# Second routing re-ordered: late tiles normalised ahead of the first half's choice, halves in turns, ScalarE's functions grouped by table

## The chip, the cores and the metric

The kernel runs on one core of a Trainium2 chip. The metric is device microseconds (us) from start to end, the median of several runs. In the text PE is TensorE, ACT is ScalarE, DVE is VectorE, POOL is GpSimd and SP the engine that issues the DMAs.

## The reference, cut to what matters

Two decoder layers over 4 x 256 = 1024 tokens of 256 features. The second layer is attention, an mLSTM, and a mixture of experts; each is added to its input and layer-normalised. The change lies in what leads from the mLSTM to the second layer's experts, 55 us of the run, and in the last heads of the mLSTM.

```python
x = _layernorm(x + mlstm(x, ctx))                         # head norm of every head, then the layer's norm
scores = softmax(x @ gate_weight.T)                       # 64 scores a token
topk_w, topk_idx = top_k(scores, 6)
w_dense = zeros((T, 64)).at[rows, topk_idx].add(topk_w)
flat = w_dense[:, inv_mapping]                            # [T, 8 experts, 8]
scalar = flat.sum(-1)
soft = softmax(where(flat == 0, -1e9, flat), axis=-1)
...
sh = silu(x @ sh_gate_W.T) * (x @ sh_up_W.T) @ sh_down_W.T   # shared expert, all tokens
return y + sh
```

## The kernel before, in words

The 1024 tokens lie in 8 tiles of 128 rows, in two halves of four tiles; four batches (0 to 3) of two tiles. The kernel writes out by hand, for every engine, the order of its instructions. Each engine works its own list strictly in that order, and waits on semaphores for the others. Work is cut into blocks, and at a block's end all engines wait for one another.

`layer1_lstm` is the block of the mLSTM: 16 heads for each of the four batches. DVE multiplies one 128 x 384 product a head (L2112) and in between does the head norm of the batch before, in steps 0 to 11 (`hn.do`). The table `AT_HEAD` says after which head which steps are done. Step 9 gives the variance (L1880), POOL raises it to the power -0.5 (`hn.power`, L1846), and steps 10 and 11 use that. Tiles 0 to 3 are finished in this block.

`layer1_route` is the block of the second routing. It has three strands, woven together.

- The late tiles: batch 3's head norm, the residual and layer norm of tiles 4 to 7 (`hn.residual`, `ln.squares` on ACT, `ln.power` on POOL, `ln.apply` on DVE at L146), then `tokens.turn` (a transpose on PE, L1917) and `tokens.keep` (ACT, L1924).
- The routing of each half: `logits` (PE, L2221), `centre` (DVE), `exp` (ACT), `choose` and `mark` (DVE, the six best), `turn_dense` (PE, L2243), `keep_dense` (ACT, L2313), `map_dense` (PE, L2251), `mask` (DVE), `exp_k` (ACT, L2317), `soften` (DVE, L2468 to L2470), `soft_copies` (ACT), `turn_soft` (PE, L2264), `keep_soft` (ACT, L2328) and `soft_rest` (DVE, L2480).
- The shared expert: six `shared_up(n)` (PE, L2231; n = 0 to 2 for the first half, 3 to 5 for the second), each followed by `silus(n)` (ACT, L2305) and `activate(n)` (DVE, L2416). `shared_up(n)` waits until `activate(n-2)` is done, since two pairs of PSUM banks go round. Then `shared_down(half)` (PE, L2272) writes the banks of the first pair, and `shared_sum(half)` (DVE, L2486) reads them. Before `shared_up(4)` PE waits for `down_read`, which `shared_sum(0)` raises.

ACT also cuts the first expert's weights into a high part (`cut_..._high`, L2594 to L2616) and POOL into a low part. Those weights are loaded by SP from the start of the block; `cut_..._high` waits for all eight loads of that expert. ACT evaluates Silu, Exp and cheap functions; `load_table` (L2332) runs a dummy call, which loads the table of the function that comes next. The block ends after `shared_down(1)` and `shared_sum(1)`, and the experts' block (`layer1_experts`) begins.

## Time and profile before

| what | value |
|---|---|
| median of 3 runs | 1106.91 us (1106.43 to 1107.95) |
| span of the profiled execution, first to last instruction | 1107.4 us |
| PE busy in it | 1003.1 us (91%) |
| DVE, ACT, POOL busy | 713.3, 606.5, 464.9 us |

The span of the profiled execution lies inside the range of the three timed runs; the profile gives no other time of its own. So what lies around the span is too small to be seen here. The times below count from the span's start. A busy PE is not PE at its peak, so what counts is where PE waits and with which clock it runs.

### The profile page before, as it was taken

How to read it: one execution, taken by the hardware profiler on the slowest of the kernel's cores; microseconds unless marked ns; L12 is line 12 of the kernel's file. 1: busy time of each engine (PE TensorE's matmuls, PEld its weight loads, DVE VectorE, ACT ScalarE, POOL GpSimd, SP SyncE). 2: the span in 40 equal slices, each digit the busy share in tenths (PEclk: the TensorE clock that was granted, in tenths of full speed). 3: DMA queues.
4: the chain of work that ended last, by engine and by line, in shares of the span. 5: the costliest groups of instructions: out<-in, count | busy, mean ns of one | idle time of the engine just before them, and what ended most of it. 6: DMA issues, size and time to landing. Idle time of an engine off the chain costs nothing. (4 is left out here: it accounts for less than half of the span.)

```text
span 1107.4 us, 18941 instructions
## 1 busy us (share of the span) xinstructions
PE 1003.1 (91%) x6066; PEld 819.1 (74%) x6066; DVE 713.3 (64%) x2102; ACT 606.5 (55%) x1650; POOL 464.9 (42%) x481
## 2 busy tenths in 40 slices
PE   7999999998995699759899999988878889999995
PEld 5899898987883599627678888964445568777884
DVE  5766666663676366546655667645787457888785
ACT  3665666555222355436576776556774555555653
POOL 5777767861377444366111110210137214443322
PEclk9999999999997799979999999988998899999998
DMA  6731111000011699624301101001003011122001
GB/s 206 257 129 67 29 30 29 21 10 1 1 53 54 200 362 337 223 84 137 103 25 62 30 20 39 1 25 50 2 1 116 0 57 58 57 71 86 17 1 38
DMA packets 83496, 85.61 MB, mean 77 GB/s; under 512 B 8545, under 2 KB 75943, under 8 KB 83280
## 3 DMA queue, kind: packets, MB, share of 16 engines
q1 hardware_dynamic: 79056, 75.39, 21.0%
q0 software_dynamic: 3072, 7.34, 2.2%
q10 hardware_dynamic: 1280, 1.77, 0.5%
q8 instruction: 47, 0.77, 0.3%
q14 instruction: 41, 0.34, 0.1%
HBM read 63.36 MB, written 22.02 MB: 77 GB/s over the span
## 5 line engine op out<-in xcount | busy, mean ns | idle before, releaser
L569 POOL TENSOR_TENSOR a_qk<-h,a_by_sin 128x512 f32<-128x512 f32 x64 | 81.7, 1277 | 5.0
L352 DVE CUSTOM_DVE_ANT_0 h<-a_score_ps,mask_bf 128x128 f32<-128x128 f32 (+1 forms) x128 | 40.8, 356 | 61.4 <-PE a_score_ps L345 61.3
L1285 POOL TENSOR_TENSOR a_w_l<-a_w,a_w_h 128x256 fp32r<-128x256 f32 x30 | 22.0, 733 | 112.7 <-ACT a_w_h L1478 112.5
L358 ACT ACTIVATE y_moe<-y_moe,a_nmax 128x128 f32<-128x128 f32 x64 | 25.6, 400 | 76.1 <-DVE a_nmax L352 76.1
L452 PEld LDWEIGHTS a_proj_ps<-a_w,xT 128*128 128x128 f32 x512 | 62.0, 192 | 3.1 <-issue 1.2
L452 PE MATMUL a_proj_ps<-a_w,xT 128*128 128x128 f32 x512 | 62.5, 276 | 0.4 <-DVE hT L510 0.4
L1024 POOL TENSOR_TENSOR e_w_l<-e_w,e_w_h 128x512 fp32r<-128x512 f32 x32 | 40.8, 1276 | 52.3 <-ACT e_w_h L1092 52.3
L80 PE MATMUL a_proj_ps<-a_x_l,a_w_h 128*128 128x512 f32 x128 | 57.4, 448 | 1.7 <-POOL a_w_l L574 1.7
L748 PE MATMUL t_y_ps<-wo,attnT 128*128 128x256 f32 x256 | 57.6, 381 | 0.0
L2628 POOL TENSOR_TENSOR m_up_l<-m_up_w,m_up_h 128x1024 fp32r<-128x1024 f32 x8 | 19.5, 2434 | 89.4 <-ACT m_up_h L2600 89.4
L352 DVE CUSTOM_DVE_ANT_0 y_moe<-a_score_ps,mask_bf 128x128 f32<-128x128 f32 (+1 forms) x128 | 40.5, 354 | 18.4 <-PE a_score_ps L345 17.0
L748 PEld LDWEIGHTS t_y_ps<-wo,attnT 128*128 128x128 f32 x256 | 47.8, 191 | 5.9
L358 ACT ACTIVATE h<-h,a_nmax 128x128 f32<-128x128 f32 x64 | 25.7, 402 | 47.8 <-DVE a_nmax L352 47.8
L82 PE MATMUL a_proj_ps<-a_x_h,a_w_l 128*128 128x512 f32 x128 | 50.6, 395 | 0.0
L81 PE MATMUL a_proj_ps<-a_x_h,a_w_h 128*128 128x512 f32 x128 | 50.0, 391 | 0.0
L506 DVE TENSOR_TENSOR h<-a_proj_ps,cos_q 128x512 f32<-128x512 f32 x32 | 22.1, 691 | 42.5 <-PE a_proj_ps L82 42.4
L510 DVE STREAM_SHUFFLE hT<-a_proj_ps 128x512 f32<-128x512 f32 x64 | 47.2, 738 | 0.0
L2112 DVE TENSOR_TENSOR wo<-l_dec,l_qk_ps 128x384 f32<-128x384 f32 x64 | 35.2, 550 | 16.0 <-ACT l_dec L2075 15.2
L565 POOL TENSOR_TENSOR a_by_sin<-hT,sin_q 128x512 f32<-128x512 f32 x32 | 41.1, 1284 | 8.0 <-DVE hT L510 7.4
L339 DVE COPY a_probsT<-a_turn_ps 128x384 f32<-128x384 f32 x64 | 34.8, 544 | 14.0 <-PE a_turn_ps L269 14.0
L565 POOL TENSOR_TENSOR a_by_sin<-hT,sin_k 128x512 f32<-128x512 f32 x32 | 41.3, 1290 | 4.4 <-DVE hT L510 4.2
L574 POOL TENSOR_TENSOR a_w_l<-a_w,a_w_h 128x256 fp32r<-128x256 f32 x30 | 21.3, 734 | 51.8 <-ACT a_w_h L600 51.7
(459 smaller groups left out, 3539.7 us busy)
## 6 DMA issues: line engine op xcount, KB each, us to landing
slots<-zeros SPq DMA_DIRECT2D x4, 2048.0 KB, 7.3
e_rows<-slots SPq DMA_DIRECT2D x32, 256.0 KB, 4.5
e_w<-in_L_ffn_w_dram SPq DMA_DIRECT2D x32, 256.0 KB, 4.7
out_slots<-e_out SPq DMA_DIRECT2D x32, 256.0 KB, 4.2
e_w<-in_L_ffn_w_dram SPq DMA_DIRECT2D x32, 128.0 KB, 4.2
a_w<-in_L_attn_w_q_dram SPq DMA_DIRECT2D x32, 128.0 KB, 2.2
m_up_w<-in_up_dram SPq DMA_DIRECT2D x8, 512.0 KB, 3.8
a_w<-in_L_attn_Wq_dram SPq DMA_DIRECT2D x16, 128.0 KB, 2.2
```

The source lines that it names most:

```text
L80: pe.matmul(out, left[0], right[1], start=start, stop=False)
L81: pe.matmul(out, left[0], right[0], start=False, stop=False)
L82: return pe.matmul(out, left[1], right[0], start=False, stop=stop)
L352: done = dve.tensor_tensor_reduce(self.probs[:, b, cells], self.score_ps[:, r, cells], self.k.mask_bf[:, cells], -1.0, 3e38, ALU.add, ALU. ...
L358: act.activation(self.probs[:, b, 0:P], self.probs[:, b, 0:P], ACT.Exp, bias=self.nmax[:, b, 0:1], scale=-1.0, accum_out=self.total[:, b, ...
L452: last = pe.matmul(proj_ps[:, c % 2, t * HD:(t + 1) * HD], k.xT[:, kc, half * HALF + t * P:half * HALF + (t + 1) * P], w[:, par, 2, kc, :] ...
L510: dve.stream_shuffle(swapped[:, r, :], proj_ps[:, c % 2, :], [i ^ 1 for i in range(32)]).then_inc(rot_in, 1)
L565: pool.tensor_tensor(by_sin[:, r2, :].rearrange("p (b s) -> p b s", b=2), swapped[:, r, :].rearrange("p (b s) -> p b s", b=2), sin[:, None ...
L569: pool.tensor_tensor(qk[:, par, 0 if what == "q" else 1, half * HALF:(half + 1) * HALF], by_cos[:, r, :], by_sin[:, r2, :], ALU.add).then_ ...
L748: last = pe.matmul(y_ps[:, t % 2, 0:D], k.ctxT[:, h, t * P:(t + 1) * P], k.wo[:, h, :], start=h == 0, stop=h == H - 1)
L1024: pool.tensor_tensor(w13_p.l[:, r], w13[:, r], w13_p.h[:, r], ALU.subtract).then_inc(w_low, 1)
L2112: dve.tensor_tensor(C[:, h % (2 * GROUP), :], dec[:, n % DECS, :], qk_ps[:, n % QK_RING, 0:CAUSAL], ALU.mult).then_inc(C_done, 1)
```

## The change: what it does

It moves instructions within the two blocks and changes no arithmetic.

- mLSTM block: `AT_HEAD` is moved up by one head, and POOL takes the power of batch 2 there rather than first in the routing block.
- Routing block: DVE finishes all late tiles ahead of `choose(0)`; PE turns all four of them behind `shared_up(2)`, then does `logits(1)` and `shared_down(0)`, and only then the first half's `turn_dense` and `map_dense`. After that the two halves alternate.
- ACT loads three tables in place of seven. Three of the weight cuts stand at its head. `silus(5)` stands behind `keep_soft(1)`.
- `turn_soft(1)` writes into `route_ps`, no longer into `turn_ps` and `x_ps`; a new semaphore `summed` guards that.

```diff
-        AT_HEAD = {9: (0, 1, 2, 3), 10: (4,), 11: (5, 6), 12: (7,), 13: (8,), 14: (9,)}
+        AT_HEAD = {8: (0, 1, 2, 3), 9: (4,), 10: (5, 6), 11: (7,), 12: (8,), 13: (9,)}
...
+                hn.power(pool, B - 2)
...
-        soft_ps = [turn_ps, x_ps]
+        soft_ps = [[turn_ps, x_ps], route_ps]
...
                 shared_up(2)
-                tokens.turn(pe, 4)
-                tokens.turn(pe, 5)
+                for t in range(EARLY, NT):
+                    tokens.turn(pe, t)
+                logits(1, (4, 5, 6, 7))
+                shared_down(0)
                 turn_dense(0)
                 map_dense(0)
-                shared_down(0)
-                tokens.turn(pe, 6)
-                tokens.turn(pe, 7)
-                logits(1, (4, 5, 6, 7))
                 shared_up(3)
-                turn_soft(0)
+                turn_dense(1)
+                map_dense(1)
                 pe.wait_ge(down_read, 2)
                 shared_up(4)
-                turn_dense(1)
-                map_dense(1)
+                turn_soft(0)
                 shared_up(5)
                 turn_soft(1)
                 shared_down(1)
...
                 load_table(ACT.Silu, 0)
-                silus(0)
+                k.ew.cut_mu_high(act, 0)
+                k.ew.cut_up_high(act, 0)
+                k.ew.cut_dqa_high(act, 0)
                 ln.squares(act, 4)
                 ln.squares(act, 5)
+                silus(0)
                 silus(1)
...
-                hn.power(pool, B - 2)
-                hn.power(pool, B - 1)
-                ln.power(pool, 4)
-                ln.power(pool, 5)
                 pool.wait_ge(loaded, N_LOADS)
...
+                hn.power(pool, B - 1)
+                for t in range(EARLY, NT):
+                    ln.power(pool, t)
...
                 activate(0)
                 centre(0)
-                activate(1)
-                choose(0)
-                ln.apply(dve, 4)
-                ln.apply(dve, 5)
-                mark(0)
                 hn.do(dve, B - 1, 10)
                 hn.do(dve, B - 1, 11)
                 hn.residual(dve, 6)
                 hn.residual(dve, 7)
+                activate(1)
+                for t in range(EARLY, NT):
+                    ln.apply(dve, t)
                 activate(2)
+                choose(0)
+                centre(1)
+                mark(0)
+                choose(1)
+                mark(1)
                 mask(0)
-                ln.apply(dve, 6)
-                ln.apply(dve, 7)
                 soften(0)
                 shared_sum(0)
-                centre(1)
-                choose(1)
-                mark(1)
-                activate(3)
-                soft_rest(0)
-                activate(4)
                 mask(1)
                 soften(1)
+                activate(3)
+                activate(4)
+                soft_rest(0)
+                soft_rest(1)
                 activate(5)
-                soft_rest(1)
                 shared_sum(1)
```

The order of PE from the third `shared_up` on, before. A row is a run of equal instructions; L2231 is the shared up projection (the first row holds n = 0 to 2, each later one a single n), L1917 the transposes of tokens, L2221 the logits, L2243 and L2251 the dense weights turned and mapped, L2264 the soft weights turned, L2272 the shared down projection.

```order
L2231 MATMUL s_up_ps<-xT,hT 128x512 x4
L2264 MATMUL s_turn_ps<-ident,s_soft 128x128 x4
L2264 MATMUL s_x_ps<-ident,s_soft 128x128 x4
L2231 MATMUL s_up_ps<-xT,hT 128x512 x4
L2243 MATMUL s_turn_ps<-ident,s_dense 128x128 x4
L2251 MATMUL s_route_ps<-s_pick,s_denseT 128x64 x4
L2231 MATMUL s_up_ps<-xT,hT 128x512 x4
L2264 MATMUL s_turn_ps<-ident,s_soft 128x128 x4
L2264 MATMUL s_x_ps<-ident,s_soft 128x128 x4
L2272 MATMUL s_up_ps<-wo,s_act 128x256 x12
```

The same stretch of PE in the changed kernel, from `shared_up(3)` to `shared_down(1)`:

```order
L2233 MATMUL s_up_ps<-xT,hT 128x512 x4
L2245 MATMUL s_turn_ps<-ident,s_dense 128x128 x4
L2253 MATMUL s_route_ps<-s_pick,s_denseT 128x64 x4
L2233 MATMUL s_up_ps<-xT,hT 128x512 x4
L2265 MATMUL s_turn_ps<-ident,s_soft 128x128 x4
L2265 MATMUL s_x_ps<-ident,s_soft 128x128 x4
L2233 MATMUL s_up_ps<-xT,hT 128x512 x4
L2265 MATMUL s_route_ps<-ident,s_soft 128x128 x8
L2273 MATMUL s_up_ps<-wo,s_act 128x256 x12
```

The second half's dense weights are now turned and mapped ahead of `shared_up(4)`, and both halves' soft weights are turned behind it.

The end of ACT's list in the routing block, before, from the copies of the second half's soft weights on (L2321, L2322 the copies, L2609 to L2616 weight cuts, L2305 the Silu of n = 5, L2328 the kept soft weights):

```order
L2321 ACTIVATE s_soft<-s_soft 128x8x32
L2322 ACTIVATE s_soft<-s_soft 128x8x32
L2609 ACTIVATE m_dqa_h<-m_dqa_w 128x256
L2614 ACTIVATE m_down_h<-m_down_w 128x256
L2616 ACTIVATE m_down_h<-m_down_s 128x256
L2305 ACTIVATE s_silu<-s_up_ps 128x512
L2328 ACTIVATE softT<-s_turn_ps 128x512
L2328 ACTIVATE softT<-s_x_ps 128x512
```

The same engine in the changed kernel, from the first half's kept dense weights (L2312) on; L2316 is `exp_k`, L2331 the table load and its dummy call:

```order
L2312 ACTIVATE s_denseT<-s_turn_ps 128x512
L2316 ACTIVATE s_expo<-s_logit 128x256
L2320 ACTIVATE s_soft<-s_soft 128x8x32
L2321 ACTIVATE s_soft<-s_soft 128x8x32
L2316 ACTIVATE s_expo<-s_logit 128x256
L2331 ACT_TABLE_LOAD
L2331 ACTIVATE s_unused<-ones 128x1
L2304 ACTIVATE s_silu<-s_up_ps 128x512
L2320 ACTIVATE s_soft<-s_soft 128x8x32
L2321 ACTIVATE s_soft<-s_soft 128x8x32
L2304 ACTIVATE s_silu<-s_up_ps 128x512
L2327 ACTIVATE softT<-s_turn_ps 128x512
L2327 ACTIVATE softT<-s_x_ps 128x512
L2327 ACTIVATE softT<-s_route_ps 128x512 x2
L2304 ACTIVATE s_silu<-s_up_ps 128x512
```

The first row here is `keep_dense(1)`, which now stands ahead of the first half's `exp_k(0)`; the last Silu moved from ahead of the kept soft weights to behind them.

## Rows read from the trace of the kernel before

**Rows 1.** The page, busy us, share of the span and instructions of each engine.

```profile
PE 1003.1 (91%) x6066; PEld 819.1 (74%) x6066; DVE 713.3 (64%) x2102; ACT 606.5 (55%) x1650; POOL 464.9 (42%) x481
```

**Rows 2.** Windows over the routing block and over the experts' block.

```profile
core 0: us, PE busy (x) PEld busy (x) DVE busy (x) ACT busy (x) POOL busy (x), PEclk, DMA share, GB/s
830.40:888.80 58.40, 50.13 (x176) 32.59 (x176) 35.18 (x99) 25.77 (x53) 26.50 (x27) 0.85 0.18 55
888.80:1107.40 218.60, 202.48 (x1056) 161.76 (x1056) 164.00 (x280) 120.00 (x229) 74.91 (x73) 0.97 0.16 49
```

**Rows 3.** Timeline of PE in the routing block: start, length, [idle before <-releaser].

```profile
834.10 12.36 PE L2231 MATMUL s_up_ps<-xT,hT 128*128 128x512 f32 x24
847.51 0.44 PE L1917 MATMUL s_x_ps<-ident,x 128*128 128x128 f32 x2 [1.05 <-DVE x L146]
...
852.52 6.59 PE L2272 MATMUL s_up_ps<-wo,s_act 128*128 128x256 f32 x24
...
861.91 3.65 PE L2231 MATMUL s_up_ps<-xT,hT 128*128 128x512 f32 x8
...
871.11 1.11 PE L2251 MATMUL s_route_ps<-s_pick,s_denseT 128*128 128x64 f32 x8 [0.80 <-ACT s_denseT L2313]
872.05 3.65 PE L2231 MATMUL s_up_ps<-xT,hT 128*128 128x512 f32 x8
877.34 0.66 PE L2264 MATMUL s_turn_ps<-ident,s_soft 128*128 128x128 f32 x4 [1.64 <-ACT s_soft L2322]
...
879.46 8.46 PE L2272 MATMUL s_up_ps<-wo,s_act 128*128 128x256 f32 x24 [1.03 <-DVE s_act L2416]
```

**Rows 4.** Windows of 2 us around the second shared down; PEclk is third from last.

```profile
876.00:878.00 2.00, 0.66 (x6) 0.66 (x7) 0.53 (x1) 1.45 (x6) 1.71 (x3) 1.00 0.00 0
882.00:884.00 2.00, 2.00 (x6) 1.55 (x6) 0.00 (x0) 0.00 (x0) 0.00 (x0) 0.50 0.00 0
886.00:888.00 2.00, 1.92 (x9) 1.33 (x8) 0.05 (x1) 0.00 (x0) 0.00 (x0) 1.00 0.00 0
```

**Rows 5.** Timeline of ACT in the routing block.

```profile
843.68 1.28 ACT L2332 ACT_TABLE_LOAD   x1
845.08 0.40 ACT L2309 ACTIVATE s_scores<-s_logit 128x256 f32<-128x256 f32 x1
...
870.46 0.59 ACT L2313 ACTIVATE s_denseT<-s_turn_ps 128x512 f32<-128x512 f32 x1
...
872.47 1.04 ACT L2600 ACTIVATE m_up_h<-m_up_w 128x1024 fp32r<-128x1024 f32 x1
...
878.11 0.57 ACT L2305 ACTIVATE s_silu<-s_up_ps 128x512 f32<-128x512 f32 x1
878.59 0.58 ACT L2328 ACTIVATE softT<-s_turn_ps 128x512 fp32r<-128x512 f32 x1
```

**Rows 6.** Timeline of DVE, last heads of the mLSTM and the routing block.

```profile
824.96 0.55 DVE L2112 TENSOR_TENSOR wo<-l_dec,l_qk_ps 128x384 f32<-128x384 f32 x1
825.42 0.18 DVE L1880 TENSOR_SCALAR hn_var<-hn_ssq 128x32 f32<-128x32 f32 x1
...
837.78 0.69 DVE L1885 TENSOR_TENSOR y_moe<-y_moe,hn_rstd 128x512 f32<-128x512 f32 x1 [2.07 <-POOL hn_rstd L1846]
...
856.87 0.42 DVE L2470 TENSOR_TENSOR s_soft<-s_expo,s_rtotal_k 128x256 f32<-128x256 f32 x1
857.21 0.69 DVE L2486 TENSOR_TENSOR y_moe<-s_up_ps,x 128x512 f32<-128x512 f32 x1
```

**Rows 7.** Timeline of ACT and POOL around the start of the routing block.

```profile
829.82 0.38 ACT L1924 ACTIVATE xT<-l_z_ps 128x256 f32<-128x256 f32 x1 [0.41 <-PE l_z_ps L1917]
830.47 1.28 ACT L2332 ACT_TABLE_LOAD   x1 [0.27 <-PEq L1965]
...
831.71 11.36 POOL L1846 TENSOR_TENSOR hn_rstd<-hn_var,minus_half 128x32 f32<-128x32 f32 x2
```

**Rows 8.** SP's issue of the first expert's last load, and its time to landing.

```profile
834.28 0.53 SPq L2570 DMA_DIRECT2D m_down_scale<-in_L_ffn_down_scale_dram  x1
...
m_down_scale<-in_L_ffn_down_scale_dram SPq DMA_DIRECT2D x1, 64.0 KB, 4.7
```

More of the change, by code:

```diff
@@ L2327, in keep_soft @@
                         act.wait_ge(soft_turned, 2 * half + side + 1)
-                        act.activation(k.softT[side][:, halves(half)], soft_ps[side][:, :], ACT.Copy
+                        act.activation(k.softT[side][:, halves(half)], soft_ps[half][side][:, :], ACT.Copy
                                        ).then_inc(soft_high, 1)
@@ L2333, in _ @@
                 load_table(ACT.Silu, 0)
-                silus(0)
+                k.ew.cut_mu_high(act, 0)
+                k.ew.cut_up_high(act, 0)
+                k.ew.cut_dqa_high(act, 0)
                 ln.squares(act, 4)
                 ln.squares(act, 5)
+                silus(0)
                 silus(1)
+                ln.squares(act, 6)
+                ln.squares(act, 7)
+                silus(2)
+                tokens.keep(act, 4)
+                tokens.keep(act, 5)
                 load_table(ACT.Exp, 1)
                 exp(0)
-                load_table(ACT.Silu, 2)
-                silus(2)
-                load_table(ACT.Exp, 3)
-                tokens.keep(act, 4)
-                tokens.keep(act, 5)
-                keep_dense(0)
-                ln.squares(act, 6)
-                ln.squares(act, 7)
-                exp_k(0)
                 tokens.keep(act, 6)
                 tokens.keep(act, 7)
+                exp(1)
+                keep_dense(0)
+                k.ew.cut_lora_high(act, 0)
+                k.ew.cut_down_high(act, 0)
+                keep_dense(1)
+                exp_k(0)
                 soft_copies(0)
-                exp(1)
-                load_table(ACT.Silu, 4)
+                exp_k(1)
+                load_table(ACT.Silu, 2)
                 silus(3)
+                soft_copies(1)
+                silus(4)
                 keep_soft(0)
-                k.ew.cut_mu_high(act, 0)
-                silus(4)
-                keep_dense(1)
-                load_table(ACT.Exp, 5)
-                k.ew.cut_up_high(act, 0)
-                k.ew.cut_lora_high(act, 0)
-                exp_k(1)
-                load_table(ACT.Silu, 6)
-                soft_copies(1)
-                k.ew.cut_dqa_high(act, 0)
-                k.ew.cut_down_high(act, 0)
+                keep_soft(1)
                 silus(5)
-                keep_soft(1)
             @block.gpsimd
@@ L2462, in mask @@
                                       ).then_inc(centred_k, 1)
-                    dve.tensor_reduce(k.scalar[:, ts, :], by_expert(routed(half)), AX, ALU.add)
+                    dve.tensor_reduce(k.scalar[:, ts, :], by_expert(routed(half)), AX, ALU.add).then_inc(summed, HT // 2)
                 def soften(half):
```

18 lines of the change are left out of this document (8 added, 10 removed).

## The prediction

> **What bounds the kernel now.** The page first: PE is busy for 91% of the span [rows 1], so in most of the run only PE's own work counts. Then the windows by block: the routing block lasts 58.40 us, PE is busy for 50.13 of them, at a mean clock of 0.85 of full [rows 2]. The experts' block behind it, 218.60 us with PE busy for 202.48, is not touched, and all engines meet between the two. So the change is worth what it moves the end of the routing block by. Third, the timeline of PE in that block [rows 3]. The reader is to see that PE always does the same matmuls and that only two things can change: the waits in square brackets, and the clock. The waits of the second half are 0.80 (map), 1.64 (soft weights) and 1.03 us (last multiply), together 3.5 us. The clock shows in the windows: full at 876 to 878, where PE waits; half at 882 to 884; full at 886 to 888 [rows 4]. It fell behind the waits of 1.64 and 1.03 us, and so the second shared down took 8.46 us where the first, of the same 24 rows, took 6.59 [rows 3]. That second shared down ends at 879.46 + 8.46 = 887.92, and this is the number that I walk the change to.
>
> **The walk through the changed order.** The queues are in order, so I lay the durations of the rows behind one another.
>
> *Start of the block.* POOL's power of batch 2 now has to end before the block can begin. Its input is ready at 825.42 + 0.18 = 825.60, and one product earlier in the new table, 825.42 - 824.96 = 0.46, so 825.14 [rows 6]. Two powers take 11.36, one 5.68 [rows 7]: it ends at 830.82. ACT, last before, ended at 829.82 + 0.38 = 830.20, and the block began at 830.47, 0.27 later [rows 7]. Now it begins at 831.09: +0.6. In return DVE no longer waits 2.07 for that power [rows 6]. I book that gain at nothing, because what comes next is not DVE.
>
> *ACT's head.* ACT now cuts weights first, and waits for their last load. It was issued at 834.28 and landed 4.7 later, at 838.98 [rows 8]; with the block 0.6 later, 839.6. The large cut takes 1.04 [rows 5], the three smaller ones about 0.3 each back to back (estimate from the 128x256 call of 0.40 [rows 5]), the two squares 0.5 each: 842.5. Then Silu 0.57 [rows 5] and DVE's multiply, as long as the 0.69 of a sum of the same size [rows 6]: 843.8. Queued behind this is the third shared up, which needs the first multiply done. Before, the three ended at 834.10 + 12.36 = 846.46 [rows 3], the last beginning 3.5 before that at 843.0. With the late start (0.6 us at half clock, so 0.3 of work) PE is there at 843.3 and waits 0.5. The third ends at 847.3, +0.8. If the weights landed 0.5 later, this would grow by as much.
>
> *From the third to the fourth shared up.* Before, 846.46 to 861.91, 15.45 us [rows 3]. PE's work in it is the same: four turns, eight logits, the first half's turn and map, and the shared down. What it waits for differs. It no longer stops twice for tokens, but once, for longer: ACT does Silu, two keeps, a table load, the exponentials and two more keeps, about 0.6 + 0.6 + 1.4 + 0.3 + 0.6 = 3.5 us, of which the turns fill 1. Waits here were 1.05 for the first tokens [rows 3] and four smaller ones; I get 3.4 after, for some 3.7 before, and book no gain. The shared down hides `centre(1)`, both `mark` and `choose(1)`, some 5 us of DVE. The fourth shared up begins at 862.7, +0.8.
>
> *The new wait ahead of `shared_up(4)`.* The fourth shared up takes 3.5 of work, to 866.2. Then the dense weights are turned (866.8), ACT keeps them, 0.59 [rows 5] (867.4), and only then does ACT do the first half's `exp_k`, 0.4 (867.8), though its input has long been there. DVE's `soften` is three operations of about 0.4 [rows 6] (869.1), and behind it in DVE's list stand the two shared sums, 0.6 apart, 0.69 each [rows 6] (870.5). PE has mapped the second half at 868.4 and stands at its wait for `down_read`: 2.0 us. This is where the gain goes: `map_dense(1)` ends at 868.4 in place of 872.2 [rows 3], 3.8 us ahead, but the fifth shared up begins at 870.5, and PE still has two shared ups and two soft turns to do, where before it had done one of each by 872.05.
>
> *The tail.* Fifth shared up to 874.0, soft turn to 874.9. The sixth waits for `activate(3)`: DVE masks the second half from 870.5, four operations of 0.42 (872.3), `exp_k(1)` 0.4, the load of Silu's table 1.4, Silu 0.57, multiply 0.69: 875.4. Sixth shared up to 878.9, second soft turn to 879.9. Now `silus(5)` stands behind both keeps of that turn, 0.58 each with some overlap [rows 5] (881.0): Silu (881.5), and the multiply behind the last `soft_rest` on DVE (882.5). Before, the last shared down began at 879.46. So it begins **3.0 us later**, behind a wait of 2.6 in place of 1.03.
>
> *The last shared down.* Its length is bounded from both sides: 6.59 (the first) and 8.46 (the second) [rows 3]. It ends at 889.1 or 891.0, +1.2 or +3.0. The wait ahead of it is long, but full-clock work stands right before it, so I take the middle, 7.5: 890.0, **+2.1 us**.
>
> *Costed at nothing.* The four removed table loads. A load and its dummy call took 845.08 - 843.68 = 1.40 us [rows 5], so 5.6 us of ACT go, but ACT is busy for 25.77 of 58.40 us [rows 2], and at the two places where PE now waits, ACT waits for PE first. The low parts of the weights on POOL, which were done well before the block's end, are so again; if they were late, the experts' first product would wait.
>
> **The skill's figure for a table load.** The row says 1.28 us for the load and 1.40 until the next function starts. The Trainium skill, page "ScalarE: Activation LUTs", section "What ACT_TABLE_LOAD costs", gives 1283 ns and a drain of about 1380 ns more, 2.66 in all. By it the four loads would free 10.6 us of ACT in place of 5.6. The load agrees with this trace, the drain does not show in it.
>
> **The sum.** Against the profiled span of 1107.4, which lies within the runs (1106.43 to 1107.95), +2.1 is 1109.5; on the median, 1106.9 + 2.1 = **1109.0**. What a measurement of this kernel can tell from no change is about 0.2%, 2.2 us: faster is below 1104.7, slower above 1109.1.
>
> **The rivals.** *The new waits, and the clock holds* (0.22). For it: the sixth shared up ends only 3.6 us before the last shared down, and the first shared down, behind the wait of 1.05 and smaller ones, took 6.59 and so lost little [rows 3]. Then the second takes no more than that, say 6.0 (estimate), and if the block also starts on time, it begins at 882.2: 888.2, +0.3, 1107.2.
>
> *The clock falls at both waits* (0.17). The 2.0 us ahead of the fifth shared up are more than the 1.64 behind which it fell [rows 3, 4]. The first three shared ups took 12.36 where three at 3.65 would take 10.95 [rows 3]; half clock so cost 1.4 there. With 0.2 of it hidden under the wait for `activate(3)`, +3.0 + 1.2 = 4.2: 1111.1. The Trainium skill, page "TensorE: Matmul & The Clock Gate", Part 1, says that the gate runs free of the kernel and that its place varies from run to run, so a new gap may cost in one version and not in the other; it gives no order between these three cases. No run here yet shows it.
>
> *Faster: the second half's lead of 3.8 us is kept* (0.08). Place: the wait ahead of `shared_up(4)`. If the shared sums were done when the map ends, PE would go on at 868.4: two shared ups and two soft turns, 8.8, then the wait of 1.03 as before and a shared down of 6.0: 884.2, -3.7, 1103.2. It decides at a wait of about 0.5 us: above that the time is no longer 0.2% better. Against it: `keep_dense(1)` stands ahead of `exp_k(0)` in ACT's list, and DVE's list has `soften(0)` ahead of the sums.
>
> *The change does nothing* (0.03): the walk's +0.8 at the start does not come and the tail's delay is made up in the experts' block, 1106.9.
>
> **How the numbers follow.** The forecast, a tail 3 us late and half lost clock, has 0.50, and its own range is 1108.1 to 1109.9, about half of it above 1109.1. Slower: 0.25 + 0.17 and a little = 0.44. Faster: 0.08. The rest, 0.48, is within 0.2%. The range reaches from 1106.0 to 1111.6; left out are the faster case and the far end of the worst.
>
> **What would show each step.** Right: PE idle about 2 us ahead of the fifth shared up, released by the shared sum; about 2.5 us ahead of the last shared down, released by DVE's multiply; ACT idle until about 839.6 ahead of its first cut; no idle time on DVE at L1885; three table loads. The block's first instruction at about 831.1. Wrong: a second shared down that begins before 880, or a fifth shared up that follows its map at once. The prediction would also fail if the clock at the start of the experts' block, which no term covers, came out otherwise.

## The result, and the profile after

The changed kernel takes **1113.55 us** (median of 4 runs, 1112.2 to 1117.36) where the kernel before, on the same chip, takes 1106.67: ratio 1.007, 95% interval 1.0046 to 1.0093. That is slower, and outside the range on record (1106.0 to 1111.6). Both were run again for the experiments; all runs of before lie between 1098.3 and 1114.3 us, 0.7% either way of their median, so one execution of one kernel tells little below that.

The profile's page of the changed kernel, first line, and windows over the routing block and over the experts' block (columns as in [rows 1, 2]):

```profile
PE 1002.5 (90%) x6066; PEld 817.3 (74%) x6066; DVE 711.1 (64%) x2102; ACT 600.4 (54%) x1642; POOL 464.5 (42%) x481
```

```profile
829.50:892.10 62.60, 52.27 (x177) 33.30 (x177) 33.63 (x99) 19.79 (x45) 21.34 (x26) 0.84 0.17 51
892.10:1110.40 218.30, 202.22 (x1056) 161.46 (x1056) 163.80 (x280) 120.03 (x229) 74.89 (x73) 0.97 0.15 49
```

The experts' block is what it was (218.60 before [rows 2]). The routing block has grown from 58.40 to 62.60: 2.1 us of it are PE busy for longer over the same matmuls, which is clock, and the rest is idle time. In the second profile of each, further down, the block took 57.03 and 59.63 us, so it grew by 2.6 there and by 4.2 here. ACT is busy 6.0 us less, which is the four table loads with their dummy calls; the block is no shorter for it.

PE in that block, changed kernel (the rows that answer to [rows 3]):

```profile
829.68 3.16 PE L2223 MATMUL s_route_ps<-wo,xT 128*128 128x64 f32 x16 [1.16 <-PEq L1965]
...
843.05 3.70 PE L2233 MATMUL s_up_ps<-xT,hT 128*128 128x512 f32 x8 [1.13 <-DVE s_act L2408]
...
850.87 3.67 PE L2223 MATMUL s_route_ps<-wo,xT 128*128 128x64 f32 x16 [1.49 <-ACT xT L1924]
854.34 6.98 PE L2273 MATMUL s_up_ps<-wo,s_act 128*128 128x256 f32 x24
...
868.22 1.10 PE L2253 MATMUL s_route_ps<-s_pick,s_denseT 128*128 128x64 f32 x8 [0.69 <-ACT s_denseT L2312]
871.02 5.40 PE L2233 MATMUL s_up_ps<-xT,hT 128*128 128x512 f32 x8 [1.70 <-DVE y_moe L2478]
...
883.89 7.13 PE L2273 MATMUL s_up_ps<-wo,s_act 128*128 128x256 f32 x24 [2.29 <-DVE s_act L2408]
```

The waits in brackets are those that the walk named: the third shared up behind the first multiply, the fifth behind the shared sum (1.70), the last shared down behind DVE's multiply (2.29). What the walk did not have is the length of the rows: 5.40 for a shared up that takes 3.65 elsewhere (5.16 in the second profile). Windows of 2 us of the changed kernel (PEclk third from last, as in [rows 4]) show why:

```profile
868.00:870.00 2.00, 1.10 (x8) 0.97 (x8) 1.43 (x4) 0.67 (x3) 0.00 (x0) 1.00 0.00 0
...
872.00:874.00 2.00, 2.00 (x4) 0.93 (x3) 1.75 (x6) 1.28 (x2) 0.00 (x0) 0.50 0.00 0
...
886.00:888.00 2.00, 2.00 (x6) 1.55 (x6) 0.00 (x0) 0.00 (x0) 0.00 (x0) 0.50 0.00 0
```

Ahead of the wait of 1.70 the granted clock is full (1.00). Behind each of the two waits it is at the lower of its two levels (1.2 GHz), not behind the last alone.

ACT's head, and DVE up to its wait for it (two timelines of the changed kernel):

```profile
838.95 0.31 ACT L2584 ACTIVATE m_rep<-m_rep_w 128x128 fp32r<-128x128 f32 x1 [7.95 <-DMA m_down_scale<-in_L_ffn_down_scale_dram]
```

```profile
834.65 0.73 DVE L1885 TENSOR_TENSOR y_moe<-y_moe,hn_rstd 128x512 f32<-128x512 f32 x1
...
842.31 0.69 DVE L2408 TENSOR_TENSOR s_act<-s_silu,s_up_ps 128x512 f32<-128x512 f32 x1 [5.02 <-ACT s_silu L2304]
```

ACT stands idle for 7.95 us before its first cut, and the DMA that ends this is the one that the walk named; DVE's wait of 2.07 at L1885 [rows 6] is gone, but it waits 5.02 for ACT's Silu instead.

**The mLSTM, which the prediction costed at next to nothing.** Windows from the first product of the mLSTM to the first table load of the routing block, one row each for the kernel before, its second run, the changed kernel and its second run:

```profile
757.56:830.47 72.91, 61.55 (x673) 33.28 (x672) 53.12 (x124) 55.94 (x170) 14.43 (x10) 0.90 0.01 1
```

```profile
759.00:828.35 69.35, 57.18 (x673) 31.09 (x672) 53.02 (x124) 55.88 (x171) 14.43 (x10) 0.97 0.01 2
```

```profile
754.24:829.50 75.26, 61.40 (x673) 33.54 (x672) 53.53 (x124) 55.77 (x171) 19.55 (x11) 0.90 0.01 1
```

```profile
758.04:834.25 76.21, 62.84 (x673) 34.40 (x672) 53.62 (x124) 55.77 (x170) 19.59 (x11) 0.88 0.01 1
```

Length less PE's busy time is PE's idle time: 11.4 and 12.2 us before, 13.9 and 13.4 after. So the new table costs PE about 2 us of idle time, in a block that the routing's rows never show. Over all twenty traces of this case it is the same: 11.0 to 12.2 us with the old table (leaving out the two in which POOL ends late), 13.4 to 14.2 with the new one or a like one. Before the mLSTM the changed kernel's profile happens to be 3.3 us ahead of before's (754.24 against 757.56), in code that both share; in the second profiles it is 1.0 (758.04 against 759.00). That lead is why the two spans (1110.4 and 1107.4) differ by less than the medians do.

### The profile page after: what moved, and what is told of

It is laid out like the page before. It is cut to its first block and busy times, and to the rows that moved or that the text cites. A ratio compares the mean times of both kernels' runs of the same rounds, so it can differ in the third digit from the quotient of the medians.

```text
span 1110.4 us, 18934 instructions
## 1 busy us (share of the span) xinstructions
PE 1002.5 (90%) x6066; PEld 817.3 (74%) x6066; DVE 711.1 (64%) x2102; ACT 600.4 (54%) x1642; POOL 464.5 (42%) x481
## 5 line engine op out<-in xcount | busy, mean ns | idle before, releaser
L352 DVE CUSTOM_DVE_ANT_0 y_moe<-a_score_ps,mask_bf 128x128 f32<-128x128 f32 (+1 forms) x128 | 40.5, 353 | 18.4 <-PE a_score_ps L345 17.1
```

The lines of the kernel that those rows point to most:

```text
L352: done = dve.tensor_tensor_reduce(self.probs[:, b, cells], self.score_ps[:, r, cells], self.k.mask_bf[:, cells], -1.0, 3e38, ALU.add, ALU. ...
```

## The experiments

Each is timed against the kernel before on the same chip. "Half clock" is the time at the lower level within a stretch, from the trace's clock record; "mLSTM" is the stretch windowed above, "block" the routing block from its first table load to the experts' first matmul.

### The two strands apart

The table and POOL's power alone, on the kernel before:

```diff
-        AT_HEAD = {9: (0, 1, 2, 3), 10: (4,), 11: (5, 6), 12: (7,), 13: (8,), 14: (9,)}
+        AT_HEAD = {8: (0, 1, 2, 3), 9: (4,), 10: (5, 6), 11: (7,), 12: (8,), 13: (9,)}
...
                 ln.power(pool, 3)
+                hn.power(pool, B - 2)
...
-                hn.power(pool, B - 2)
                 hn.power(pool, B - 1)
```

> The kernel before with only the mLSTM part of the change: AT_HEAD moved up by one head, and POOL's power of batch 2 taken there. Theory A (this part costs as well; product by product, the traces show the stretch of 64 products about 3 us longer in the changed kernel, after they had run side by side): 2 to 4 us slower than before, and in the trace the gaps behind the products of heads 8 and 14 of batches 2 and 3 are longer by about 1 us each. Rival B (the whole loss is in the routing block, the rest is where the clock happens to fall): within 1 us of before. Rival C (it gains: DVE no longer waits 2.07 us for the power): 1 to 2 us faster.

Measured: 1109.49, ratio 1.0042 (1.0019 to 1.0065). The lesser half of the change, booked at +0.6 us, costs 4.2 us between the medians; the interval leaves 2 to 7 us. Theory A had said 2 to 4.

The changed kernel with these lines put back (the routing block's order alone):

> The changed kernel with the mLSTM block as it was before, and the power of batch 2 back at the head of POOL's list in the routing block. Theory A (two parts that add up): 3 to 5 us slower than before, with the routing block at 61 to 63 us in place of 58.4. Rival B (all of the loss is here): 6 to 8 us slower. Rival C (the loss is all in the mLSTM): within 1 us of before.

Measured: 1111.68, ratio 1.0065 (1.004 to 1.0089). That is rival B's size. The two do not add up to the whole (1.007, and 1.0054 again below): without the power in the mLSTM, POOL does both powers in the block, and the late tokens' turn waits 2.69 us where the changed kernel waits 0.52. So this run does not price the routing order as it stands in the changed kernel, and taking the table back out of that kernel alone was not timed.

The table without POOL's power (first hunk alone), one profile:

> The kernel before with only AT_HEAD moved up by one head; POOL takes the power of batch 2 in the routing block as before. Theory A (the table makes the mLSTM longer: DVE has four steps, two residual operations and a copy behind head 8 in one piece, PE's next products wait for it and ACT behind PE): the mLSTM stretch is 74.5 to 75.5 us as with both parts, with gaps of about 2.1 us behind heads 8 and 9 of batches 2 and 3. Rival (POOL's power, which now has to end before the block does, makes it longer): 72 to 73 us.

Measured: 1111.34, mLSTM 74.96 us, in line with 74.85 with the power, both at 15 us of half clock; the kernel before, at 15 too, had 72.91. So it is the table that makes this stretch longer, by some 2 us at an equal clock, and not POOL's power.

### How far one profile can be trusted

The kernel before, unchanged, profiled and timed again, and the changed kernel likewise:

> The kernel before, unchanged, once more. Theory A says that its first profile was a slow sample: the PE of the changed kernel was 2.9 us ahead of it by the second layer's attention, in code that both share. So this one's span should be 1103 to 1107 us, with the 2.9 us gone or in another place, and its routing block again 57 to 60 us. Rival (the 2.9 us come from the change in some way): the span is 1107 us again and the changed kernel keeps its lead there.

> The changed kernel, unchanged, on the same chip as the others. Theory A (two parts, +2.3 us in the mLSTM and +4 to 5 in the routing block): mLSTM stretch 74.5 to 75.5 us, routing block 61 to 64 us, 6 to 9 us slower than before. Rival (part of the first result was chance): 3 us or less slower.

Measured: before against before 1.0017 (0.9992 to 1.0043), so nothing; changed 1112.99, 1.0054 (1.0036 to 1.0073), so the result stands. The changed kernel's block came out at 59.63 us and its mLSTM at 76.21, both outside what was expected of them, at 17.1 and 19.0 us of half clock. Rows of the second shared down in three traces with the same order and the same wait of 1.03: before [rows 3] 8.46, and

```profile
877.47 6.86 PE L2272 MATMUL s_up_ps<-wo,s_act 128*128 128x256 f32 x24 [1.03 <-DVE s_act L2416]
```

in its second run, and in the kernel with another table (empty_end, below)

```profile
882.44 5.45 PE L2272 MATMUL s_up_ps<-wo,s_act 128*128 128x256 f32 x24 [1.03 <-DVE s_act L2416]
```

Same waits, 3 us apart by clock alone. The row of 8.46, on which the prediction bounded its last term, was the longest of the second shared downs in all twenty traces; the others took 5.35 to 7.13.

### Where the table loses its time

The first guess was the pile of steps behind head 8; the second, that heads 14 and 15 have nothing left behind them. Three other tables on the kernel before, power left in the block:

```diff
+        AT_HEAD = {8: (0,), 9: (1, 2, 3, 4), 10: (5, 6), 11: (7,), 12: (8,), 13: (9,)}   # spread
+        AT_HEAD = {8: (0, 1, 2, 3), 10: (4,), 11: (5, 6), 12: (7,), 13: (8,), 14: (9,)}  # pile8
+        AT_HEAD = {9: (0, 1, 2, 3, 4), 10: (5, 6), 11: (7,), 12: (8,), 13: (9,)}         # empty_end
```

> As e7, but of the four first steps only step 0 stands behind head 8, and steps 1 to 4 behind head 9; the later steps one head up as in the change. Theory A in its first form (the pile behind head 8 costs): the gap behind head 8 shrinks to about 1.3 us and the stretch is 1 us shorter than in e7. Second form (what costs is that DVE has nothing left to do behind heads 14 and 15, and waits there for ACT, whatever the split): the stretch is as long as in e7, 74.5 to 75.5 us.

> The kernel before with only the first four steps of the head norm moved from behind head 9 to behind head 8; steps 4 to 9 stay where they were, so heads 14 and 15 have as much behind them as before. Theory 'the pile': the gap behind head 8 is 2.1 us (1.0 to 1.1 before) in each of three batches, and the mLSTM part is 2 us longer than 72.7 us at equal half clock, ratio 1.002. Theory 'the empty end': the gap behind head 8 grows, but the gaps behind heads 9 and 10 shrink by as much, heads 14 and 15 keep 0.55 and 0.67, and the mLSTM part stays within 0.7 us of 72.7 at equal half clock; ratio 0.999 to 1.002.

> The kernel before with head 8 left as it was, and steps 4 to 9 of the head norm moved up by one head, so that nothing is left behind head 14. Theory 'the empty end': the gaps behind heads 14 and 15 become 0.95 to 2.5 and 0.8 to 1.3 us as in the changed kernel, and the mLSTM part is 1.5 to 2.5 us longer than 72.7 us at equal half clock, ratio 1.002 to 1.004. Theory 'the pile': the gaps behind heads 14 and 15 stay at 0.55 and 0.67 and the part at 72.7, ratio 1.000.

Measured: spread 1112.27 (one run), mLSTM 77.64, longer than either form of its theory said; pile8 1105.54, ratio 1.000 (0.9972 to 1.0028), mLSTM 69.26; empty_end 1110.36, ratio 1.0046 (1.0019 to 1.0072), mLSTM 77.77. The pile falls. On one chip empty_end is slower than pile8 by 4.8 us between the medians. But an empty end only names where DVE then waits; the traces say why. Timeline of DVE from head 8's product on (batch 2), second run of before:

```profile
798.19 0.56 DVE L2112 TENSOR_TENSOR wo<-l_dec,l_qk_ps 128x384 f32<-128x384 f32 x1
...
799.27 0.55 DVE L2112 TENSOR_TENSOR wo<-l_dec,l_qk_ps 128x384 f32<-128x384 f32 x1
...
800.70 0.49 DVE L2112 TENSOR_TENSOR wo<-l_dec,l_qk_ps 128x384 f32<-128x384 f32 x1
801.11 0.68 DVE L1866 TENSOR_TENSOR y_moe<-cT,hn_rnorm 128x512 f32<-128x512 f32 x1
801.83 0.69 DVE L1870 TENSOR_REDUCE hn_hsum<-y_moe 128x32 f32<-128x512 f32 x1
802.43 0.55 DVE L2112 TENSOR_TENSOR wo<-l_dec,l_qk_ps 128x384 f32<-128x384 f32 x1
```

and PE's mixing of heads 8 to 11 in it:

```profile
804.00 0.86 PE L2020 MATMUL l_hT_ps<-wo,l_v_b 128*32 128x128 f32 x24
```

The same in the changed kernel:

```profile
795.44 0.56 DVE L2113 TENSOR_TENSOR wo<-l_dec,l_qk_ps 128x384 f32<-128x384 f32 x1
...
799.40 0.54 DVE L2113 TENSOR_TENSOR wo<-l_dec,l_qk_ps 128x384 f32<-128x384 f32 x1
799.86 0.17 DVE L1872 TENSOR_SCALAR hn_nmu<-hn_hsum 128x32 f32<-128x32 f32 x1
800.07 0.69 DVE L1874 TENSOR_TENSOR cT<-y_moe,hn_nmu 128x512 f32<-128x512 f32 x1
800.67 0.55 DVE L2113 TENSOR_TENSOR wo<-l_dec,l_qk_ps 128x384 f32<-128x384 f32 x1
```

```profile
802.25 0.93 PE L2021 MATMUL l_hT_ps<-wo,l_v_b 128*32 128x128 f32 x24
```

Head 11 closes a group of four, and PE mixes the group only when that product is done: in both, 1.57 us behind its start (804.00 - 802.43; 802.25 - 800.67, 1.58), and in no trace less. From head 8's product to head 11's it is 802.43 - 798.19 = 4.24 before and 800.67 - 795.44 = 5.23 now, because steps 5 and 6 (0.17 and 0.69) have moved ahead of head 11's product. The windows over these two stretches (columns as in [rows 2]):

```profile
798.19:802.43 4.24, 2.98 (x40) 1.56 (x38) 4.07 (x15) 3.36 (x12) 1.03 (x2) 1.00 0.01 2
```

```profile
795.44:800.67 5.23, 2.88 (x40) 1.65 (x38) 4.99 (x16) 3.79 (x13) 0.79 (x2) 1.00 0.00 2
```

DVE is busy nearly throughout in both (4.07 and 4.99 us), and PE, at full clock, idles for 1.26 and 2.35 us. Behind head 11's product the room that DVE has gained behind heads 13 to 15 is of no use. By this reading the loss is whatever the table adds ahead of head 11:

| table | head 8 to head 11, batches 1, 2, 3 | PE idle there, sum | mLSTM | PE idle in it | half clock in it |
|---|---|---|---|---|---|
| before, second run | 4.32, 4.24, 4.17 | 3.4 | 69.35 | 12.2 | 4.5 |
| pile8 | 3.70, 4.42, 4.35 | 3.4 | 69.26 | 12.1 | 4.6 |
| changed | 4.51, 5.23, 5.15 | 5.8 | 75.26 | 13.9 | 14.5 |
| spread | 5.07, 5.24, 5.16 | 6.2 | 77.64 | 13.9 | 21.4 |
| empty_end | 5.32, 5.23, 5.16 | 6.4 | 77.77 | 14.2 | 21.4 |

pile8, which moves only what lies behind heads 8 and 9 and leaves steps 5 and 6 behind head 11, is as fast as before; every table with them ahead of it is slow. Each of those tables also leaves head 14 with nothing behind it, so the timings can't tell head 11 from the empty end. The traces can, for the idle time: between the products of heads 8 and 11 PE idles 3.4 us in all twelve traces with the old table or pile8, and 5.8 to 6.4 in all eight others, while from the product of head 12 on it idles 2.6 to 3.0 us in the eight and 2.5 to 5.0 in the twelve. What waits longer behind heads 14 and 15 is DVE, and mostly at half clock.

The lengths in the table are not at an equal clock. The idle time (+2 us) is less than half of the difference in length. The rest is clock: the windows of pile8 and empty_end,

```profile
754.90:824.16 69.26, 57.17 (x673) 31.44 (x672) 53.17 (x124) 55.56 (x170) 15.42 (x10) 0.97 0.01 2
```

```profile
755.89:833.66 77.77, 63.56 (x673) 34.67 (x672) 53.93 (x124) 55.58 (x171) 14.36 (x10) 0.86 0.01 1
```

have PE busy for 57.17 and 63.56 us over the same 673 matmuls. Half clock in the stretch was 4.5 to 18.1 us in twelve traces with old-like tables (mean 10.5) and 14.5 to 21.4 in eight with the late head 11 (mean 17.0). Among the old ones that start the next block on time, the length grows by 0.35 us per us of half clock (69.35 at 4.5, 74.13 at 18.14), so 6.5 us more of it are worth 2.3 us. Together with the 2 us of idle time that makes 4.3, next to the 4.2 between the medians. Only the idle time is the same in every trace: the clock's part is an estimate from ranges that overlap, and the interval of the timing (from 2 us on) would allow the idle time alone. The rule of head 11 was not the expectation of any run, and no table was run that moves steps 5 and 6 and keeps work behind head 14.

### The waits of the routing block, one by one

Two edits against the waits in the changed kernel (sums), with the tables of the change:

```diff
-                keep_dense(1)
                 exp_k(0)
+                keep_dense(1)
...
-                soften(0)
                 shared_sum(0)
+                soften(0)
```

> The changed kernel with the wait ahead of the fifth shared up taken away: on ACT exp_k(0) ahead of keep_dense(1), on DVE shared_sum(0) ahead of soften(0). All else as in the changed kernel. Theory A (that wait of 1.70 us, and the half clock behind it, 5.40 in place of 3.65 us, are on the path): 1.5 to 3.5 us faster than the changed kernel. Rival (the sixth shared up waits for activate(3) anyway and the tail takes it back): less than 0.7 us faster, with the same time longer in front of the sixth shared up.

Measured: 1113.65, ratio 1.0086 (1.006 to 1.0113): no gain. In its trace the wait ahead of the fifth shared up is gone and that row takes 3.65 again, but 0.70 us are new ahead of the sixth, and ahead of the last shared down PE still waits 2.28. The wait ahead of the third shared up has grown to 3.03; it lies ahead of the edit, and PE reaches it earlier there because the first two shared ups took 8.29 us in place of 9.28. This trace has 6.8 us of half clock in the block and is one of the two fastest of nine runs (1107.87), so it does not show what the median pays; that stays open.

The tail alone, on the routing order alone:

```diff
-                keep_soft(1)
                 silus(5)
+                keep_soft(1)
...
-                soft_rest(1)
                 activate(5)
+                soft_rest(1)
```

> The kernel with the routing block's new order alone, and one more edit: the last shared ups' SwiGLU is issued on VectorE and ScalarE ahead of the second half's softened weights, so that the last shared down isn't kept waiting for its operand. In the trace of the routing block alone TensorE waits 2.29 us there. Theory 'single waits': that wait falls to about 1 us, the routing block is 1 to 1.5 us shorter than in that kernel (63.2 us by its trace) at equal half clock, and the ratio to the kernel before falls from 1.0065 to about 1.005. Rival 'the map's turn takes it': the wait goes to the turn of the second map or to the experts' first products, which get their softened weights later; no change, ratio 1.006 or above.

Measured: 1108.96, ratio 1.002 (1.0002 to 1.0038), against 1.0065 without the edit and 1.005 expected. The last shared down in its trace:

```profile
882.97 5.45 PE L2272 MATMUL s_up_ps<-wo,s_act 128*128 128x256 f32 x24 [0.60 <-DVE s_act L2408]
```

The wait is 0.60 for 2.29. That is 1.7 us; the timing gave more than twice as much, and the rest I can't attribute: the intervals of the two ratios leave some 1.5 to 8 us for the edit.

The head (ACT's three cuts behind `silus(1)`), on the routing order alone:

> The kernel with the routing block's new order alone, and one more edit: ScalarE's three cuts of weights stand behind the second pair's sigmoid instead of ahead of it. Theory 'single waits': the wait ahead of the third shared up (0.20 us in the trace of the routing block alone, 1.13 us in the changed kernel's, 3.03 us in that with the two sums moved) is gone whatever the clock does at the block's start, and the ratio to the kernel before falls from 1.0065 to between 1.003 and 1.0055. Rival 'the cuts are late instead': the first product that reads the cut shared down weights waits for them and the ratio stays at 1.006 or above.

Measured: 1112.25, ratio 1.0057 (1.0036 to 1.0078), no change that shows. The wait ahead of the third shared up is not gone, and the late tokens behind it come at their time, behind POOL's two powers, whatever ACT does: their turn starts 19.2 us behind the block's first table load here and in the trace without the edit.

```profile
836.71 3.70 PE L2232 MATMUL s_up_ps<-xT,hT 128*128 128x512 f32 x8 [1.03 <-DVE s_act L2408]
844.07 0.69 PE L1917 MATMUL s_x_ps<-ident,x 128*128 128x128 f32 x2 [3.66 <-DVE x L146]
```

Tail and sums together, and all three:

> The kernel with the routing block's new order alone, with two edits: the last multiply ahead of the last softened weights (the tail), and the first half's exponentials and shared sum each one place up (the sums). Theory 'single waits': both waits are gone (1.70 us ahead of the fifth shared up, most of 2.29 us ahead of the last shared down), the ratio is 0.999 to 1.001, as with all three edits. Rival 'the sums give nothing': the ratio stays at 1.002, that of the tail edit alone.

> The changed routing with the mLSTM block as it was before, and all three new waits taken away: the weight cuts on ACT behind silus(1); exp_k(0) ahead of keep_dense(1) and shared_sum(0) ahead of soften(0); silus(5) ahead of keep_soft(1) and activate(5) ahead of soft_rest(1). Theory A (the loss of the routing block is these waits and the half clock behind them): the routing block takes 55 to 58 us, 0 to 3 us faster than before. Rival (the re-ordering itself holds PE back, behind the third shared up, where the four tokens are turned at once and the clock is lost): routing block 59 us or more, 1 to 4 us slower than before.

Measured: 1.0021 (0.9987 to 1.0055), which fits either theory, and 1.0004 (0.9983 to 1.0025). All three bring the routing order back to the time before, not below it. Which of the sums and the head gives the last 0.2%, if it is there, is inside the intervals.

### The clock by itself

Products on PE that compute nothing that is read (the kernel's own helper `keep_clock`, 512 columns each, two matmuls in the trace), put where PE waits. In the changed kernel eight: one ahead of `logits(1)`, two ahead of the wait for `down_read`, two ahead of `shared_down(1)`, three at the experts' start (the expectation names the first shared down for the second place; the edit sets them ahead of the fifth shared up). In the kernel before five:

```diff
                 shared_up(5)
+                keep_clock(pe, x_ps[:, :], k.ident[:, :], k.xT[:, 0, 0:HALF], 1)
                 turn_soft(1)
+                pe.wait_ge(act_done, 2 * SH_TILES - 1)
+                keep_clock(pe, up_ps[:, 0, :], k.ident[:, :], k.xT[:, 0, 0:HALF], 1)
                 shared_down(1)
...
                 low_inputs(0)
+                keep_clock(pe, gu_ps[:, 0, :], k.ident[:, :], k.xT[:, 0, 0:HALF], 3)
                 factors(0)
```

> The changed kernel with eight products added on TensorE that compute nothing that is read (512 columns each): one ahead of the logits of the second half, two ahead of the first shared down, two ahead of the last, three at the start of the experts. They stand where TensorE waits anyway. Theory 'the clock carries a good part of the routing block's loss': half clock in the block falls from 17 to 20 us to under 12 us, and the kernel is 1.5 to 4 us faster than the changed one (ratio to the kernel before 1.002 to 1.005 where the changed kernel had 1.0054 to 1.007). Rival 'the waits alone': the half clock may change, the time doesn't, ratio 1.0055 to 1.008; if the fillers delay what stands behind them, 2 us slower yet.

> The kernel before with five products added on TensorE that compute nothing that is read (512 columns each): one ahead of the turn of the second half's softened weights, one ahead of the last shared down, three at the start of the experts. It is the candidate for a version that beats both. Theory 'the clock': half clock in the routing block falls from 14 to 17 us to under 12 us, ratio to the kernel before 0.997 to 0.999. Rival: the clock doesn't answer to so few products, or they delay what stands behind them by as much as they save: 0.9995 to 1.003.

Measured: changed kernel with eight, 1107.30, ratio 1.0017 (0.9995 to 1.0039), 5.7 us below its second timing and beyond the 1.5 to 4 expected; half clock in the block 3.4 us where two traces of it had 20.5 and 17.1. Kernel before with five, **1101.85, ratio 0.9965** (0.9946 to 0.9983): faster than both, and a little more than expected. Its tail:

```profile
871.48 1.02 PE L89 MATMUL s_x_ps<-xT,ident 128*128 128x512 f32 x2
873.29 0.66 PE L2264 MATMUL s_turn_ps<-ident,s_soft 128*128 128x128 f32 x4 [0.78 <-ACT s_soft L2325]
873.78 0.60 PE L2264 MATMUL s_x_ps<-ident,s_soft 128*128 128x128 f32 x4
874.22 1.02 PE L89 MATMUL s_up_ps<-xT,ident 128*128 128x512 f32 x2
875.41 5.45 PE L2272 MATMUL s_up_ps<-wo,s_act 128*128 128x256 f32 x24 [0.17 <-DVE s_act L2419]
```

The added rows lie where the waits of 1.64 and 1.03 stood [rows 3], delay nothing, and the last shared down takes 5.45 us. By itself this row proves little, since empty_end has 5.45 there without any added product, and three traces without them had less half clock in the block (10.2 us) than this one (11.0). What does show it: the second run of before has the same rows to within 0.05 us from the block's start up to the first added product, and then 6.86 for 5.45 and an experts' stretch of 219.5 us for 217.1. That stretch is 217.1 to 217.2 us in all four traces with three products at its start, 218.2 to 219.7 in all sixteen without. And over all timed runs the mean granted clock is 0.959 to 0.962 in the four kernels with added products, 0.950 to 0.957 in all others.

### What the new order is worth once mended

On the routing order alone, with the tail edit and seven added products:

> The kernel with the routing block's new order alone, the tail edit, and seven added products that compute nothing that is read (one ahead of the second half's logits, two ahead of the fifth shared up, one ahead of the last shared down, three at the start of the experts). Theory 'waits and clock add up': half clock in the routing block under 6 us, the block's length 54 to 55.5 us, ratio 0.996 to 0.9985. Rival 'the new order stays behind': its waits on the way, hidden or not, keep it above the kernel before with its five added products, ratio 0.999 to 1.002.

Measured: 1106.60, ratio 1.0007 (0.9978 to 1.0037); the rival holds. In its trace the block took 58.9 us with 13.7 at half clock, not 54 to 55.5 with under 6: added products do not hold the clock everywhere. The late tokens come 19.2 us behind the block's start here too, behind POOL's two powers.

The changed kernel with the old table, POOL's power kept in the mLSTM block, tail and sums mended; and that with five added products:

> The changed kernel with the old table of head-norm steps, POOL's power of batch 2 kept in the mLSTM block, and the two edits against its waits (first half's exponentials and shared sum one place up, last multiply ahead of the last softened weights). Theory 'these three are the loss': the routing block is 54.5 to 56 us long and the mLSTM part 72.7 us at equal half clock, ratio 0.997 to 1.000; against the changed kernel (1.0054 to 1.007) 0.7% faster. Rival 'more is lost elsewhere': the ratio stays at 1.001 or above, with the late start of the block (0.8 us, POOL's power ends after ACT) or the wait of the late tokens as the place.

> The same kernel with five added products that compute nothing that is read (one ahead of the second half's logits, one ahead of the last shared down, three at the start of the experts). Theory: the clock adds to the waits, ratio 0.994 to 0.997, better than the kernel before with its five added products (0.9965). Rival: the new order leaves fewer gaps that half clock follows, so that the added products give under 0.1% and the ratio is that of the kernel without them, or 0.997 and above.

Measured: 1107.00, ratio 1.0014 (0.9988 to 1.0041), and **1102.30, ratio 0.9959** (0.9941 to 0.9977). In the first the routing block took 55.9 us and has 6.9 us of PE idle where before has 8.4, and yet it gains nothing: with the old table POOL's power ends after ACT, and the block starts late.

```profile
826.98 5.43 POOL L1846 TENSOR_TENSOR hn_rstd<-hn_var,minus_half 128x32 f32<-128x32 f32 x1 [1.99 <-DVE hn_var L1880]
```

```profile
832.91 3.37 PE L2223 MATMUL s_route_ps<-wo,xT 128*128 128x64 f32 x16 [2.44 <-PEq L1965]
```

The power ends at 832.41, and PE stands 2.44 us at the block's start where before stands 0.88, about what the block has saved; the changed kernel stands 1.16. Moving the table up saves 1.3 us here and costs about 4. In the second, with the products, the block took 52.4 us against 55.6 in the kernel before with five, and the mLSTM 72.3 against 69.4, 1.6 of it this late start (one trace each). With the added products the new order (0.9959) and the old (0.9965) can't be told apart: all of the gain is the products', none shown to be the order's.

## Why the prediction was wrong

**The failed step is "Start of the block"**, as the only cost of the mLSTM strand: +0.6 us for POOL's power, and nothing for the table, without a reason. The prediction takes from the table only that the power's input is ready one product earlier, and says that the change is worth what it moves the end of the routing block by. The power cost 0.3 at most (PE's wait at the block's start, 1.16 for 0.88 in the first profile, 0.88 again in the second). The table costs about 2 us of PE's idle time, ahead of head 11, and by estimate as much in clock; this strand by itself is 1.0042, 4.6 us (2 to 7). In place of the 0.6 in the forecast of 1109.0 that gives 1113.0, measured 1113.55 and 1112.99. That it comes so close is luck, at intervals of this width. I had taken a row of DVE's list as moved work of known size, and did not ask who waits for the product that it was moved ahead of.

**The routing block was walked nearly right, but its clock was not.** Wait by wait, predicted and measured in the first profile: third shared up 0.5 and 1.13 (none in the second); fifth 2.0 and 1.70; last shared down 2.6 and 2.29; last shared down's length 7.5 and 7.13; the block's start +0.6 and +0.3. ACT's first cut 8.5 us behind the block's start, and 9.45 (8.29 in the second). PE, from the block's start to the last shared down: 882.5 - 831.09 = 51.4 walked; 883.89 - 829.50 = 54.4 in the first profile and 51.4 in the second. The 3 us between them are rows at half clock that the walk took at full: 5.40 for 3.65 behind the wait for the sum, 3.67 for 2.00 in the second logits, 6.98 for the first shared down. The second profile has less of it (5.16, 2.71, 6.39), and its equality with the walk is luck, since the walk had the fifth shared up at full clock. So in both profiles the clock falls behind both waits, as the rival "the clock falls at both waits" (0.17) says. In length, from the block's start to the end of the last shared down, the first (61.5) is the rival's 61.0, and the second (58.6) the forecast's 58.9.

**The sum against its own profile.** "What lies around the span is too small to be seen" was wrong: each run shows 1.8 to 1.9 us more than its span (1112.2 against 1110.4). So the execution profiled before took some 1109.3 us, above all three runs listed, and its routing block (58.5, half clock 17.6) was 1.5 us longer than in the second run (57.03, half clock 14.5). A walk measured from its end hides that much of a loss. The medians, which the forecast also used, do not have this fault (1106.91 and 1106.67).

**Right as stated**: three table loads; no idle time at L1885 and no gain that shows from it; the place and size of the wait for the shared sum; the experts' block unchanged. That the table loads gave nothing is not shown by a run of its own, and "this is where the gain goes" is not either: the run that took this wait away was no faster. Of the slow start of a kernel's matmuls, the Trainium skill, page "TensorE: Matmul & The Clock Gate", Part 1, says that the gate's window runs free and that the result is run-variable. In the middle of this kernel the traces agree, with 8.46, 6.86 and 5.45 us for the same 24 matmuls behind the same wait.

**Open.** Why the tail edit gave more than its 1.7 us; why the edit of the sums gave nothing; and what of the routing order's 7 us (1.0065) is each wait's; three edits together recover it, and the single ones can't be resolved at intervals of 0.4%. The late tokens behind POOL's two powers are part of it: in two traces that differ in this alone their turn starts 17.0 us behind the block's start with one power in the mLSTM, and 19.2 with both in the block. Whether PE's longer idle time in the mLSTM causes its half clock there, or the traces only happen to fall so, was not tried with added products in that block.

## What to carry to other kernels

When filler work moves in an in-order queue, ask what it moves ahead of: an item that closes a group for another engine is worth more than its neighbours, and room gained behind it was worth nothing here. Cost both blocks that a diff touches, the small hunk too: a table of numbers is an order. And before polishing an order around waits of 1 to 2 us on TensorE, try products that compute nothing in them: here five gave 0.35%, and no re-ordering without them was faster than before.

## What the runs showed of the hardware

- Executions of the kernel before lie 0.7% either way of their median (1098.3 to 1114.3 us), most of it with the granted clock: over the runs of one kernel the span falls by 0.35 to 0.94 us, in most of the kernels by 0.5 to 0.8, for each 0.001 of mean granted clock.
- A us at half clock cost 0.35 us in the mLSTM, from 69.35 us with 4.5 at half clock to 74.13 with 18.1; the trace has PE idle for 11 to 12 us of this stretch.
- Behind waits of 1.03, 1.70 and 2.29 us the granted clock fell to its lower level in some traces; in others the same waits of 1.03 and 2.29 were followed by a shared down of 5.45 us.
- Three added products at the experts' start (2.74 us in all, in a stretch where PE waits 2.10) went with an experts' stretch of 217.1 or 217.2 us in four traces, in place of 218.2 or more in sixteen. With seven added products the routing block of another order still had 13.7 us at half clock.
- A table load took 1.28 us wherever it stood, and where the next function was ready, that one began 1.40 us behind the load's start.
